# A fused conv and feed-forward block on one core: the pipeline's first three steps put in another order

## The chip, the core and the metric

The kernel runs on one core of a Trainium2 chip. The metric is the device time of one execution in microseconds (us); of several runs the median counts. Six engines work side by side, each with its own instruction stream, and meet only at semaphores: TensorE (PE, with its weight loads as PEld), VectorE (DVE), ScalarE (ACT), GpSimd (POOL) and SyncE (SP). SP and ACT issue the transfers; "SPq" and "ACTq" in a row stand for such issues.

## The reference

For an image batch x of 4 x 48 x 128 x 128 (channels second):

```
x = x + conv(ln_c(x))          # ln_c: mean and variance over the 48 channels of a pixel
  conv: 3x3 conv of the first 12 channels, 1x1 conv 48 -> 254,
        rfft2 of each 8x8 patch * fft_w, irfft2,
        gelu(first 127) * (last 127), 1x1 conv 127 -> 48
t = tokens(x)                  # one token for each pixel
t = t + ffn(ln_t(t))           # 48 -> 192, relu, 192 -> 48, operands rounded to fp8 (5 exponent, 2 mantissa bits)
```

## The kernel before, in words

The work is cut into 32 steps (`STEPS`), each of 16 image rows. A step's data run through a pipeline of seven stages written out in `step(t)` of every engine: a call of `step` for turn a does stage 0 for chunk a, stage 1 for chunk a-1, and so on up to stage 6. So the first turns are a filling in which most stages are not live. In this text turn a is the call for chunk a; (n) behind a name is the chunk.

What a chunk goes through in its first three turns:

- **Stage 0.** SP loads x(n) into `xin` (two slots, so x(2) needs x(0) to be used up), in two halves of 48 channels (`load_x`, L342). ACT copies it in patch order into the single buffer `xord` (`order_x`, L934). PE turns it to pixels in `bank[0]` and `bank[1]` (eight transposes, L784). ACT reads the two banks as `xpix` (L1068) and squares (L1071). DVE makes sums, mean and variance `st` (L1435 to L1459). POOL takes the power -1/2 (`pow`, L1555), copies it to `rm` (L1559), centres the pixels (`centre`, `xcen`, L1530) and scales them into `zpix` (L1572).
- **Scaling of the 12 conv channels.** They lie in another layout (`cx`). For the first three chunks DVE spreads the statistics (`widen_rows`, `tch`, L1193), PE multiplies with masks (`spread(a)`, L595), and DVE applies the result to `cx` (`early_channels`, `cz`, L1206 to L1215). Later chunks get them by way of DRAM (`rm_scratch`).
- **Stages 1 and 2.** SP stores `cz` to DRAM (`store_channels`, L308), into rows between zero rows (`pads`, stored by ACT at the start, L941), and reads it back shifted as `taps` (`load_taps`, L333 and L335). PE does the 3x3 conv (`stream`, L568), ACT copies it out (`convs`, L1114), PE turns it (`convolve`, L577), ACT writes it into `zpix` (L1122).
- **Stage 3.** PE transforms (`fwd`, L803), ACT and DVE split the result into fp16 parts `zh` and `zl`, PE mixes channels (`mix`, L519) and transforms back (`inverse`, L532 and L539), with `gelu` on ACT and `gate` on DVE. Stages 4 to 6 are the projection and the feed-forward part.

The weights are loaded by SP in the same queue and turned by PE in turn 2 (`setup`, L493 to L503). Matmuls on the identity (`keep_busy`, L583) have no use but to occupy PE. The order of work is written out by hand on every engine; each engine stands still at the first wait that is not met. Around the change it is this. PE in turn 2: turn x(2), `spread(1)`, weight setup, 16 `keep_busy`, `stream(0)`, 2 `keep_busy`, `convolve(0)`, `spread(2)`; turn 3 begins with turning x(3), then the transform of chunk 0. SP in turn 2: stores, `cx`, `taps`, then x(3), then biases. POOL in turn 0: power, then `rm`; `centre(0)` follows in turn 1.

Of the kernel before, what the change touches and what calls it, by code (L numbers as in the profile page):

```python
# [80 lines left out]
def metaformer_kernel(nc, x, w_pc, w_in, fft_w, w_out, w1, b1, w2, b2, fwd_d, inv_d, sel_d, eye_d, out):  # L81
    with ExitStack() as ctx:
# [120 lines left out]
        small_set = sem("small_set")  # L203
        zeroed = sem("zeroed")
# [89 lines left out]
        tiles = lambda t: t.rearrange("p (r i w) -> p i r w", r=PATCH, w=TW)  # L294

# [42 lines left out]
        def _(sp):  # L338
# [16 lines left out]

            sp.dma_start(eye[:], eye_d).then_inc(eye_in, 16)
            load_x((0, 0), 0)
            load_cx((0, 0), 0)
            load_x((0, 0), -1)
# [58 lines left out]
            def step(t):  # L418
# [68 lines left out]
        def _(pe):  # L487
# [272 lines left out]

            def step(t):
# [14 lines left out]
                if live(t, 0):  # L776

                    if not peeled:
                        pe.wait_ge(hid16_ready, upto(6 * l + 5))
                    if peeled and a == 0:  # L780
                        pe.wait_ge(eye_in, 16)
                    pe.wait_ge(xord_ready, upto(a + 1))
                    for i in range(PAIRS):
                        mm = pe.transpose(bank[i // 4][:, (i % 4) * 128:(i % 4) * 128 + XSPAN],  # L784
                                          xord[:, i * PX:(i + 1) * PX], eye[0:XSPAN, 0:XSPAN])
                        if i % 4 == 3:
                            mm.then_inc(xT_done, 1)
# [96 lines left out]
        def _(act):  # L884
# [30 lines left out]
            def layers():  # L915

                act.wait_ge(wT, 1)
                act.wait_ge(set_dve, 12 + 4)
# [11 lines left out]
            def order_x(t, behind):  # L930
# [3 lines left out]
                act.activation(xord[:].rearrange("p (i r w) -> p i r w", r=PATCH, w=TW),  # L934
                                tiles(xin[:, ring(t, behind), :]), ACT.Copy).then_inc(xord_ready, 1)

            act.wait_ge(row_zeroed, 1)
            for part in range(2):
                for r in (0, PR - 1):
                    images = cz_d[part].rearrange("c (b r) w -> c b r w", b=BATCH)  # L940
                    act.dma_start(images[:, :, r, :], zero_row[0:CC, :].unsqueeze(1).to_broadcast([CC, BATCH, PW]))\  # L941
                      .then_inc(pads_out, 16)
# [114 lines left out]

            def step(t):
                a, n, m, k, l = (at(t, d) for d in (0, 3, 4, 5, 6))
                filling = isinstance(t[0], int) and t[1] < 3  # L1060
                if live(t, 0):
                    for q in range(2):
                        act.wait_ge(xT_done, upto(2 * a + q + 1))
                        if q == 0:
                            act.wait_ge(xcen_ready, upto(a - 1))
                            act.wait_ge(sum1, upto(a - 1))
                        src = bank[q][:].rearrange("p (i c) -> p i c", c=128)[:, :, 0:XSPAN]
                        act.activation(xpix[:, ring(t, 0), 4 * q:4 * q + 4, :], src, ACT.Copy).then_inc(xpix_ready, 1)  # L1068
                        act.wait_ge(stat1, upto(4 * a))
                        act.sem_inc(act_held, 1)  # L1070
# [579 lines left out]
```

## Time and profile before

| | us |
|---|---|
| median of 3 runs (lowest, highest) | 699.83 (699.67, 700.46) |
| span of the profiled execution | 699.4 |
| PE busy | 666.5 (95% of the span) |
| DVE, ACT, POOL busy | 597.9, 536.8, 456.9 |

The times are of whole executions, the profile is of one more. Its page cuts the span in 40 slices; in the slices' row of PE the first four read 4, 8, 7 and 9 tenths busy, all from there to the last three read 9 (90% or more). So what PE leaves idle lies in the first 70 us or so and at the very end.

### The profile page before, as it was taken

To read this page: it belongs to the slowest core of one execution; us is meant where nothing else is said; L and a number is where in the kernel's file an instruction comes from. 1 tells how busy PE (TensorE), PEld (TensorE's weight loads), DVE (VectorE), ACT (ScalarE), POOL (GpSimd) and SP (SyncE) were. 2 spreads that over 40 slices of the span, in tenths; PEclk is the share of its full clock that TensorE was granted. 3 is DMA by queue.
4 is the path that set the end of the run, shared out by engine and by line. 5 is a ranking of instruction groups with operands and counts; after the bars stand their busy time and mean duration, and the time that the engine had idled before them with its cause. 6 is when DMAs were issued, how large, how long until landed. Compare 5 with 4: busy or idle time off the path is not lost.

```text
span 699.4 us, 19176 instructions
## 1 busy us (share of the span) xinstructions
PE 666.5 (95%) x6620; PEld 529.3 (76%) x6620; DVE 597.9 (85%) x1159; ACT 536.8 (77%) x1087; POOL 456.9 (65%) x347
## 2 busy tenths in 40 slices
PE   4879999999999999999999999999999999999984
PEld 4657877778778877787878877787788777887751
DVE  7637889988988899988988899889888999877877
ACT  4244568888888888888889888888888888877784
POOL 2605677767777777677776877677777876753353
PEclk9989999999999999999999999999999999999995
DMA  4434445444544554445444544545445543342102
GB/s 102 79 78 118 121 113 131 112 126 128 142 120 118 142 140 121 114 120 138 127 123 131 139 131 107 132 121 144 121 116 144 139 129 103 100 119 87 47 23 68
DMA packets 52207, 80.73 MB, mean 115 GB/s; under 512 B 20823, under 2 KB 36079, under 8 KB 52111
## 3 DMA queue, kind: packets, MB, share of 16 engines
q1 hardware_dynamic: 50031, 78.56, 43.2%
q10 hardware_dynamic: 2080, 0.94, 0.6%
q8 instruction: 54, 0.88, 0.6%
q14 instruction: 42, 0.34, 0.2%
HBM read 63.17 MB, written 16.30 MB: 114 GB/s over the span
## 4 chain that ended last, share of the span: by engine, by line
PE 87%; DVE 3%; DMA 3%; issue 2%; ACT 1%; SPq 1%; POOL 1%; DVEq 0%; ACTq 0%; POOLq 0%
PE inva L532 17%; PE invb L539 15%; PE mixp L519 13%; PE misc L548 8%; PE misc L803 8%; PE misc L619 4%; PE misc L519 4%; PE misc L663 3%; PE misc L784 3%; PE misc L568 2%; PE misc L577 2%; PE misc L653 2%; PE mixp L632 2%; PE mixp L639 2%; DMA xin<-in_x_dram 1%
## 5 line engine op out<-in xcount | busy, mean ns | idle before, releaser
L1555 POOL TENSOR_TENSOR st<-st,neg_half 128x16 f32<-128x16 f32 x32 | 93.3, 2915 | 129.2 <-DVE st L1459 129.2
L532 PEld LDWEIGHTS inva<-inv,gmix 128*127 128x127 f32 x1024 | 123.4, 191 | 25.3 <-issue 16.6
L532 PE MATMUL inva<-inv,gmix 128*127 128x128 f32 x1024 | 141.0, 281 | 0.6 <-DVE gmix L1234 0.6
L1234 DVE TENSOR_TENSOR gmix<-mixp,freq_w 128x508 f32<-128x508 f32 x192 | 122.6, 680 | 16.9 <-PE mixp L519 16.9
L539 PE MATMUL invb<-inv,gmix 128*127 128x128 f32 x1024 | 134.7, 274 | 0.1
L539 PEld LDWEIGHTS invb<-inv,gmix 128*127 128x127 f32 x1024 | 126.2, 191 | 2.1 <-DVE hbuf L1245 0.5
L897 ACT ACTIVATE hid<-misc 128x512 f16<-128x512 f32 x180 | 94.1, 599 | 17.7 <-PE misc L619 17.7
L1245 DVE TENSOR_TENSOR hbuf<-gact,invb 127x512 f32<-127x512 f32 x128 | 87.4, 683 | 22.2 <-ACT gact L889 17.7
L1584 POOL TENSOR_TENSOR st<-st,neg_half 128x16 f32<-128x16 f32 x31 | 95.4, 3077 | 16.4 <-DVE st L1313 15.9
L906 ACT ACTIVATE hid<-hid 128x512 fp8e5<-128x512 f16 x174 | 93.2, 619 | 0.0
L889 ACT ACTIVATE gact<-inva 127x512 f32<-127x512 f32 x128 | 77.5, 605 | 19.9 <-PE inva L532 19.3
L519 PE MATMUL mixp<-win,zh 60*128 60x254 f16 x768 | 89.9, 272 | 0.7 <-DVE gmix L1234 0.6
L519 PE MATMUL mixp<-win,zl 60*128 60x254 f16 x768 | 89.0, 267 | 0.0
L1538 POOL TENSOR_TENSOR ob<-tch,y 112x1024 f32<-112x1024 f32 x29 | 62.1, 2140 | 34.1 <-DVE y L1294 34.1
L977 ACT ACTIVATE y<-mixp 112x512 f16<-112x512 f32 x58 | 31.4, 594 | 47.0 <-PE mixp L639 47.0
L803 PE MATMUL misc<-fwd,zpix 128*124 128x128 f32 x512 | 62.1, 275 | 0.0
L548 PE MATMUL misc<-hbuf,wout 127*64 127x512 f32 x248 | 60.1, 605 | 0.0
L803 PEld LDWEIGHTS misc<-fwd,zpix 128*124 128x124 f32 x512 | 58.6, 188 | 0.0
L519 PEld LDWEIGHTS mixp<-win,zh 60*128 60x128 f16 x768 | 37.1, 93 | 26.8 <-issue 14.5
L1435 DVE TENSOR_REDUCE st<-xpix 128x16 f32<-128x768 f32 x32 | 30.5, 952 | 28.3 <-ACT xpix L1068 28.3
L1580 POOL TENSOR_TENSOR tcen<-tpix,st 128x768 f32<-128x768 f32 x31 | 45.7, 1475 | 12.5 <-DVE st L1301 9.6
L1068 ACT ACTIVATE xpix<-misc 128x384 f32<-128x384 f32 x64 | 31.6, 494 | 23.2 <-PE misc L784 22.1
(184 smaller groups left out, 1358.2 us busy)
## 6 DMA issues: line engine op xcount, KB each, us to landing
taps<-cz_scratch SPq DMA_DIRECT2D x63, 292.2 KB
xin<-in_x_dram SPq DMA_DIRECT2D x64, 192.0 KB, 3.3
xres<-in_x_dram SPq DMA_DIRECT2D x64, 192.0 KB, 4.1
out_dram<-ob SPq DMA_DIRECT2D x60, 192.0 KB, 2.6
taps<-cz_scratch SPq DMA_DIRECT2D x63, 146.1 KB
crm<-rm_scratch SPq DMA_DIRECT2D x58, 96.0 KB
cx<-in_x_dram SPq DMA_DIRECT2D x32, 96.0 KB
cz_scratch<-cz SPq DMA_DIRECT2D x63, 48.8 KB
```

The costliest lines, as they stand in the source:

```text
L519: mm = pe.matmul(pair[q][:, e * HID2:(e + 1) * HID2], zpart[r0:r0 + KC, 2 * s + e, :], win[r0:r0 + KC, wpart, :], start=(e == 0 and zpart ...
L532: mm = pe.matmul(inva[0:HID, q * PX:(q + 1) * PX], gmix[:, s % 2, q, 0:HID], inv[:], start=True, stop=True, skip_group_check=True)
L539: mm = pe.matmul(invb[0:HID, q * PX:(q + 1) * PX], gmix[:, s % 2, q, HID:HID2], inv[:], start=True, stop=True, skip_group_check=True)
L548: mm = pe.matmul(dst[HALF * j:HALF * j + HALF, :], wout[:], hbuf[:, half, j, :, :], start=True, stop=True, skip_group_check=True)
L803: mm = pe.matmul(bank[(3, 0)[i // 4]][0:KSPAN, (i % 4) * PX:(i % 4 + 1) * PX], zpix[:, ring(t, 3), i, 0:KSPAN], fwd[:], start=True, stop=True,
L889: act.activation(gact[:, s % 2], inva[0:HID, :], ACT.Gelu).then_inc(gelu_ready, 1)
L897: act.activation(hid16[:, 3 * c + g, :], bank[g][:], ACT.Copy).then_inc(hid16_ready, 1)
L906: act.activation(hid8[:, 3 * c + g, :], hid16[:, 3 * c + g, :], ACT.Copy, saturate=False)\
L1234: dve.tensor_tensor(gmix[:, s % 2, 2 * q:2 * q + 2, 0:HID2], pair[q][:, 0:2 * HID2].rearrange("p (e c) -> p e c", e=2), freq_w[:], ALU.mul ...
L1245: dve.tensor_tensor(hbuf[:, s // 2, :, 2 * e:2 * e + 2, :], gact[:, s % 2].rearrange("p (j i c) -> p j i c", j=2, i=2), invb[0:HID, :].rea ...
L1555: pool.tensor_tensor(st1[:, 6, :], st1[:, 5, :], neg_half[:], ALU.pow).then_inc(pow1, 1)
L1584: pool.tensor_tensor(st2[:, 6, :], st2[:, 5, :], neg_half[:], ALU.pow).then_inc(pow2, 1)
```

## The change

It touches only the first turns (0 to 3) and what stands ahead of them.

- Ahead of turn 0: SP loads the first half of x(0), then the identity, then the first half of x(1). ACT issues the second halves. ACT then does a `Gelu` on 8 elements and only then orders x(0). The zero rows (`pads`) are stored by ACT in turn 1.
- `zpix` is zeroed by POOL, not by DVE.
- x(1) is put in patch order by DVE (`order_second_x`), ahead of its statistics of chunk 0; ACT orders x(0) and x(2), x(3) and on.
- POOL does `centre(0)` ahead of the first power. The copy to `rm` in turns 1 and 2 waits for `spread_in` (the widened rows are written), not for the matmuls on them.
- x(3) is loaded by SP in turn 1, ahead of the stores of `cz`.
- PE in turn 2: 12 `keep_busy`, `spread(2)`, `stream(0)`, turning of x(3), `convolve(0)`. Turn 3 begins with the transform.
- ACT in turn 3: first half of the pixels, `zh` half 0, second half of the pixels, `zh` half 1. DVE in turn 3: `zl` half 0 ahead of the sum over x(3).

```
@@ sync, ahead of turn 0
-            load_x((0, 0), 0)
+            load_first_half(0)
             sp.dma_start(eye[:], eye_d)...
+            load_first_half(1)
             load_cx((0, 0), 0)
-            load_x((0, 0), -1)
@@ sync, step
                     if a == 0:
                         setup()
+                        sp.wait_ge(xord_ready, 2)
+                        load_x((0, 2), -1)
...
-                if a == 2:
-                    sp.wait_ge(xord_ready, 2)
-                    load_x(t, -1)
@@ tensor, step
-                    for i in range(PAIRS): ... transpose ...
+                    if a != 3:
+                        turn_x(t)
...
                 if a == 2:
-                    keep_busy(16, bank[1])
+                    keep_busy(12, bank[1])
+                    spread(2)
                 if live(t, 2):
                     stream(t)
-                    if peeled and a == 2:
-                        keep_busy(2, bank[1])
+                    if a == 2:
+                        turn_x((0, 3))
...
                     convolve(t)
-                    if peeled and a == 2:
-                        spread(2)
@@ scalar, ahead of turn 0
+            load_second_half(0)
+            load_second_half(1)
             act.wait_ge(row_zeroed, 1)
-            (four stores of zero rows)
+            act.activation(gact[0:1, 0, 0:8], zero_row[0:1, 0:8], ACT.Gelu)...
             order_x((0, 0), 0)
@@ scalar, step
+                        if a == 3 and q == 0:
+                            pixels(t, 1)
...
-                if live(t, -1):
+                if live(t, -1) and a != 0:
                     order_x(t, -1)
+                if a == 1:
+                    pads()
@@ vector
-            for tile in (raw_b, cz16, xres, zpix, qpix, win, wout, l1, l2, wpc):
+            for tile in (raw_b, cz16, xres, qpix, win, wout, l1, l2, wpc):
...
+            def order_second_x():
+                dve.wait_ge(x_in[1], 32)
+                dve.wait_ge(xT_done, 2)
+                dve.tensor_copy(strips(xord), tiles(xin[:, 1, :])).then_inc(xord_ready, 1)
+
+            order_second_x()
...
+                if a == 3:
+                    low_parts(t, 0)
@@ gpsimd
-                if a == 1:
-                    centre(t, 1)
+                if a == 0:
+                    centre(t, 0)
...
-                    pool.wait_ge(rmT_done, upto(a))
+                    if a in (1, 2):
+                        pool.wait_ge(spread_in, a)
+                    else:
+                        pool.wait_ge(rmT_done, upto(a))
...
+            pool.memset(zpix[:], 0.0).then_inc(zpix_zeroed, 1)
```

Below are the rows of the instruction order at three places; the rows are program order and tell no times.

PE from the second set of masks (`spread(1)` ends just above) to the transform of chunk 0. `misc<-tch` is `spread(2)`, `misc<-eye,xord` the turning of x(3). Before:

```order
L583 MATMUL misc<-eye 128x128 x16
L568 MATMUL misc<-taps,wpc 32x512 x8
L583 MATMUL misc<-eye 128x128 x2
L577 MATMUL misc<-eye,convs 128x128 x4
L595 MATMUL misc<-tch 96x2x128 x4
L784 MATMUL misc<-eye,xord 128x96 x8
L803 MATMUL misc<-fwd,zpix 124x128 x8
```

And with the change:

```order
L588 MATMUL misc<-eye 128x128 x12
L600 MATMUL misc<-tch 96x2x128 x4
L573 MATMUL misc<-taps,wpc 32x512 x8
L775 MATMUL misc<-eye,xord 128x96 x8
L582 MATMUL misc<-eye,convs 128x128 x4
L813 MATMUL misc<-fwd,zpix 124x128 x8
```

`spread(2)` moved ahead of the stream, and the turning of x(3) moved from behind `spread(2)` to between stream and `convolve`.

POOL in turns 0 and 1. `st<-st,neg_half` is the power. Before:

```order
L1555 TENSOR_TENSOR st<-st,neg_half 128x16
L1559 COPY rm<-st 128x16
L1530 TENSOR_TENSOR xcen<-xpix,st 128x576
L1555 TENSOR_TENSOR st<-st,neg_half 128x16
L1559 COPY rm<-st 128x16
```

And with the change:

```order
L1661 MEMSET zpix 128x2048
L1569 ISA
L1569 TENSOR_TENSOR xcen<-xpix,st 128x576
L1594 TENSOR_TENSOR st<-st,neg_half 128x16
L1601 COPY rm<-st 128x16
L1594 TENSOR_TENSOR st<-st,neg_half 128x16
L1601 COPY rm<-st 128x16
```

The centring of chunk 0 no longer stands between the two powers.

SP from the last weight load to the loads of turn 3. Before:

```order
L380 DMA raw_pc<-in_L_conv_w_pc_dram 36x12x1 x6
L308 DMA cz_scratch<-cz 12x8x260 x3
L347 DMA cx<-in_x_dram 96x1x256
L333 DMA taps<-cz_scratch 72x1x2078
L335 DMA taps<-cz_scratch 36x1x2078
L342 DMA xin<-in_x_dram 48x1024 x2
L386 DMA raw_b<-in_L_ffn_b_dram 128x1
```

And with the change:

```order
L386 DMA raw_pc<-in_L_conv_w_pc_dram 36x12x1 x6
L345 DMA xin<-in_x_dram 48x1024 x2
L311 DMA cz_scratch<-cz 12x8x260 x3
L350 DMA cx<-in_x_dram 96x1x256
L336 DMA taps<-cz_scratch 72x1x2078
L338 DMA taps<-cz_scratch 36x1x2078
L392 DMA raw_b<-in_L_ffn_b_dram 128x1
```

The load of x(3) moved from behind the `taps` to ahead of the stores.

## Rows read from the trace of the kernel before

**Rows 1.** Windows: us, busy us of each engine, PEclk, DMA share, GB/s.

```profile
29.00:33.50 4.50, 4.50 (x25) 4.27 (x24) 3.53 (x11) 2.00 (x10) 4.31 (x4) 0.62 0.60 167
...
39.50:46.60 7.10, 5.92 (x22) 4.72 (x23) 1.11 (x3) 2.33 (x5) 0.00 (x0) 0.52 0.17 42
...
107.00:126.00 19.00, 19.00 (x193) 15.23 (x191) 17.07 (x34) 15.93 (x34) 14.52 (x11) 1.00 0.51 132
```

**Rows 2.** The chain that ended last, 28 to 50 us: start, us, what.

```profile
29.73 0.79 SPq L335
...
31.31 7.76 DMA xin<-in_x_dram
...
39.09 1.06 ACT xord L934
...
40.69 1.11 PE misc L577 x4
41.80 3.41 PE misc L595 x8
45.21 1.28 PE misc L784 x8
46.49 1.91 PE misc L803 x16
48.41 1.34 PE misc L583 x12
```

**Rows 3.** Timeline, 30 to 38 us: start, us, engine, line, operation [idle before].

```profile
31.77 1.55 DVE L1193 TENSOR_TENSOR tch<-rm,tch 128x512 f32<-128x512 f32 x1 [0.23 <-POOL rm L1559]
...
37.17 0.65 PE L568 MATMUL misc<-taps,wpc 108*32 108x512 f16 x8 [2.48 <-DMA taps<-cz_scratch]
```

**Rows 4.** Timeline, 58 to 62 us: the same stages one turn later.

```profile
58.51 0.65 PE L568 MATMUL misc<-taps,wpc 108*32 108x512 f16 x8
...
59.21 0.60 ACT L1114 ACTIVATE convs<-misc 128x512 f32<-128x512 f32 x1 [1.13 <-PE misc L568]
...
60.06 0.66 PE L577 MATMUL misc<-eye,convs 128*128 128x128 f32 x4
...
60.76 0.49 ACT L1122 ACTIVATE zpix<-misc 128x384 f32<-128x384 f32 x1 [0.95 <-PE misc L577]
```

**Rows 5.** Timeline, 0 to 7 us: loads and ACT.

```profile
0.74 0.40 SPq L356 DMA_DIRECT2D eye<-in_identity_dram  x1
...
1.20 0.88 SPq L342 DMA_DIRECT2D xin<-in_x_dram  x2
...
4.84 1.28 ACT L934 ACT_TABLE_LOAD   x1 [4.84 <-issue]
...
6.14 1.06 ACT L934 ACTIVATE xord<-xin 96x1024 f32<-96x1024 f32 x1
```

**Rows 6.** The tile xin, 0 to 60 us: its transfers' time from issue.

```profile
DMA to landing us min/median/max: 3.0/4.2/7.8
```

**Rows 7.** Timeline, 7 to 24 us: PE, DVE and POOL.

```profile
9.63 0.95 DVE L1435 TENSOR_REDUCE st<-xpix 128x16 f32<-128x768 f32 x1 [1.06 <-ACT xpix L1068]
...
10.95 1.51 PE L784 MATMUL misc<-eye,xord 96*128 96x96 f32 x8 [2.10 <-ACT xord L934]
...
12.33 2.92 POOL L1555 TENSOR_TENSOR st<-st,neg_half 128x16 f32<-128x16 f32 x1 [11.89 <-DVE st L1459]
...
15.63 1.15 POOL L1530 TENSOR_TENSOR xcen<-xpix,st 128x576 f32<-128x576 f32 x1
15.64 1.17 DVE L1459 TENSOR_SCALAR st<-st 128x16 f32<-128x16 f32 x1
...
16.96 3.41 POOL L1555 TENSOR_TENSOR st<-st,neg_half 128x16 f32<-128x16 f32 x1 [0.18 <-DVE st L1459]
...
21.61 1.97 PE L595 MATMUL misc<-tch 128*96 128x256 f32 x8 [1.31 <-DVE tch L1193]
```

**Rows 8.** The chain again, 72 to 78 us.

```profile
72.95 4.41 DMA taps<-cz_scratch
```

More of the change, by code:

```diff
@@ L203, in metaformer_kernel @@
         small_set = sem("small_set")
+        zpix_zeroed = sem("zpix_zeroed")
+        table_in = sem("table_in")
         zeroed = sem("zeroed")
@@ L759, in drain, with turn_x @@
                 second_layer_half(1, invb)
+            def turn_x(t):
+                a, l = at(t, 0), at(t, 6)
+                if FIRST <= t[1] < LAST:
+                    pe.wait_ge(hid16_ready, upto(6 * l + 5))
+                elif a == 0:
+                    pe.wait_ge(eye_in, 16)
+                pe.wait_ge(xord_ready, upto(a + 1))
+                for i in range(PAIRS):
+                    mm = pe.transpose(bank[i // 4][:, (i % 4) * 128:(i % 4) * 128 + XSPAN],
+                                      xord[:, i * PX:(i + 1) * PX], eye[0:XSPAN, 0:XSPAN])
+                    if i % 4 == 3:
+                        mm.then_inc(xT_done, 1)
             def step(t):
@@ L776, in step @@
                 if live(t, 0):
[L778 to L787, printed above, removed]
+                    if a != 3:
+                        turn_x(t)
                     if a == 1:
@@ L917, in layers @@
                 act.wait_ge(wT, 1)
-                act.wait_ge(set_dve, 12 + 4)
+                act.wait_ge(set_dve, 11 + 4)
                 for j in range(2):
@@ L933, in order_x, with load_second_half, pads @@
                 act.wait_ge(xT_done, upto(2 * a))
-                act.activation(xord[:].rearrange("p (i r w) -> p i r w", r=PATCH, w=TW),
+                act.activation(strips(xord),
                                 tiles(xin[:, ring(t, behind), :]), ACT.Copy).then_inc(xord_ready, 1)
-            act.wait_ge(row_zeroed, 1)
[L938 to L942, printed above, removed]
+            def load_second_half(n):
+                act.dma_start(xin[CH:2 * CH, n, :], xv[0, n, 1]).then_inc(x_in[n], 16)
+            def pads():
+                for part in range(2):
+                    for r in (0, PR - 1):
+                        images = cz_d[part].rearrange("c (b r) w -> c b r w", b=BATCH)
+                        act.dma_start(images[:, :, r, :], zero_row[0:CC, :].unsqueeze(1).to_broadcast([CC, BATCH, PW]))\
+                          .then_inc(pads_out, 16)
+            load_second_half(0)
+            load_second_half(1)
+            act.wait_ge(row_zeroed, 1)
+            act.activation(gact[0:1, 0, 0:8], zero_row[0:1, 0:8], ACT.Gelu).then_inc(table_in, 1)
             order_x((0, 0), 0)
@@ L1056, in drain, with pixels @@
                            .then_inc(out_stored, 16)
+            def pixels(t, q):
+                a = at(t, 0)
+                act.wait_ge(xT_done, upto(2 * a + q + 1))
+                if q == 0:
+                    act.wait_ge(xcen_ready, upto(a - 1))
+                    act.wait_ge(sum1, upto(a - 1))
+                src = bank[q][:].rearrange("p (i c) -> p i c", c=128)[:, :, 0:XSPAN]
+                act.activation(xpix[:, ring(t, 0), 4 * q:4 * q + 4, :], src, ACT.Copy).then_inc(xpix_ready, 1)
+                act.wait_ge(stat1, upto(4 * a))
+                act.sem_inc(act_held, 1)
+                act.activation(xsq[:, 8 * q:8 * q + 8, :].rearrange("p (i j) c -> p i (j c)", j=2), src, ACT.Square).then_inc(xsq_ready, 1)
             def step(t):
@@ L1060, in step @@
                 filling = isinstance(t[0], int) and t[1] < 3
[L1061 to L1070, printed above, removed]
-                        act.activation(xsq[:, 8 * q:8 * q + 8, :].rearrange("p (i j) c -> p i (j c)", j=2), src, ACT.Square).then_inc(xsq_ready, 1)
+                if live(t, 0) and a != 3:
+                    pixels(t, 0)
+                    pixels(t, 1)
+                if a == 3:
+                    pixels(t, 0)
                 if filling and t[1] == 2:
@@ L1085, in step @@
                                        bank[(3, 0)[q]][0:KSPAN, :], ACT.Copy).then_inc(hi_ready, 1)
+                        if a == 3 and q == 0:
+                            pixels(t, 1)
                 if live(t, 4):
@@ L1127, in setup @@
                 act.wait_ge(zeroed, 1)
+                act.wait_ge(zpix_zeroed, 1)
             run(act, step, setup, 1)
@@ L1167, in setup @@
                 dve.tensor_copy(eye8[:], eye[:], saturate=False).then_inc(set_dve, 1)
-                dve.wait_ge(set_dve, 12 + 5)
+                dve.wait_ge(set_dve, 11 + 5)
                 for base in (0, HALF):
@@ L1182, in late_setup @@
                 dve.tensor_copy(b8[:], raw_b[:], saturate=False).then_inc(set_dve, 1)
[L1183 removed]
+                dve.wait_ge(set_dve, 11 + 11)
                 dve.tensor_copy(bq[:], b8[:]).then_inc(set_dve, 1)
@@ L1186, in late_setup @@
                 dve.tensor_copy(l1h[:], l1[:]).then_inc(set_done, 1)
-                dve.wait_ge(set_dve, 12 + 12)
+                dve.wait_ge(set_dve, 11 + 12)
             def widen_rows(a):
@@ L1429, in step @@
                     early_channels(1)
+                if a == 3:
+                    low_parts(t, 0)
                 if live(t, 0):
@@ L1436, in step @@
                 if live(t, 3):
-                    low_parts(t, 0)
+                    if a != 3:
+                        low_parts(t, 0)
                     low_parts(t, 1)
@@ L1622, in setup @@
                 pool.wait_ge(zeroed, 1)
+                pool.wait_ge(zpix_zeroed, 1)
             run(pool, step, setup, 1)
```

10 lines of the change are left out of this document (6 added, 4 removed).

## The prediction

> **What bounds the kernel now.** I first read the table of busy times over stretches. Between 107 and 126 us PE is busy 19.00 of 19.00 us at a granted clock of 1.00 [rows 1]: from there to the drain the time is PE's work, and this change does not touch that work. So whatever the filling loses or gains moves everything behind it, and the question is only when the full steps begin. I take as that moment the first `mix` of chunk 0, which starts at about 49.7 us (the row of 48.41 us ends there, [rows 2]).
>
> Next I read the chain of what ended last, backwards from that moment, because it names what each engine waited for. It runs, in order: the `taps` issues on SP, the load of x(3) queued behind them (7.76 us from issue, landing at 39.07), ACT ordering x(3), then on PE `convolve` 1.11, `spread(2)` 3.41, turning x(3) 1.28, the transform 1.91 and `keep_busy` 1.34 us [rows 2]. Yet the taps themselves were there at 37.17, when the stream began [rows 3]. From the stream to the first mix thus pass 12.5 us, and most of it is not needed for chunk 0: it is work for x(3) and chunk 2 that stands in the way.
>
> Last I read the first 24 us as a timeline. Each chunk's statistics end in a power of about 3 us on POOL, and two of these in a row, with a centring between them, lead to `spread(1)` at 21.61 [rows 7]. Everything to the stores of `cz` and the issue of the `taps` follows from there.
>
> I call T the start of `stream(0)`, 37.17 us before. The change has three parts: what comes before `spread(1)`, what comes from there to T, and what comes from T to the first mix.
>
> **Part one, up to spread(1).** ACT orders x(0) at 6.14, right as its table load ends (4.84 + 1.28 = 6.12) [rows 5]; that load stood behind four stores of zero rows. After the change two x issues and the table load are over well before x(0) is there, so x(0)'s landing decides. SP's x issues took 0.44 us each [rows 5]; landing takes 3.0 us at least and 4.2 in the median [rows 6]. With the first issue at 0.74 that is 3.7 to 4.9. I take 4.2, near the low end, since nothing is ahead of it in the queues: 1.9 us gained, bounds 1.2 and 2.4. The trace does not show when x(0) landed before, as the table load covers it; at 1.20 + 3.0 = 4.2 it can have been there, so the gain is the cover taken away and hardly the second queue.
>
> The Trainium skill has a rule against the second queue here (DMA: Bandwidth & Descriptors, its decision table): spreading transfers over issuing engines gives no bandwidth, they share the same 16 DMA engines, and only issue time is saved. By that rule the two halves on ACT are worth their issue time alone; a view in which two queues doubled the rate would put the landing near 3 us and the end another 1 us lower. No row here separates the two.
>
> DVE now orders x(1) ahead of its statistics of chunk 0. ACT's copy of the same shape takes 1.06 us [rows 5]; for DVE I take the same as the upper bound and half of it as the lower. It can start once PE has turned x(0): 4.2 + 1.06 of ordering + 1.51 for eight transposes [rows 7] and a hand-over, so DVE is at it from about 6.9 to 8.0. The sums would be ready to start at 9.63 - 1.9 = 7.7 [rows 7], so DVE starts them at 8.0: 1.6 us gained, and the first power moves from 12.33 to 10.7. That x(1) lands by 6.9 is plausible (issued by 2.1, plus 4.2) with 0.6 us to spare.
>
> The second power began 4.63 us after the first (12.33 to 16.96): 2.92 of power, the copy, then the centring of 1.15 us, in which DVE's last small operation of the statistics took 1.17 us in place of 0.17 [rows 7]. With the centring ahead of the first power, what lies between is the power and a copy with their hand-overs, 3.5 us: the second starts at 14.2, a gain of 2.8. The statistics of chunk 1 are no later: PE turns x(1) at 8.1 where it was 10.95 [rows 7], 2.9 us sooner. The centring now runs while DVE sums squares and is done at 10.2; if it holds up one small DVE operation, that costs 0.3. `spread(1)` thus starts at 18.8. Edits that cost nothing here: POOL's zeroing of `zpix` (POOL was idle 11.89 us before its first power; 1.15 us for 576 elements scales to 4.1 us for 2048) and the zero rows on ACT, which lie in its wait for x(2)'s pixels; if they ran over, only the statistics of chunk 2 would feel it, and these wait for DVE.
>
> **Part two, from spread(1) to T.** The stores and the `taps` issues keep their distance to `spread(1)`: 2.8 us sooner. The last issue ended at 30.52 (29.73 + 0.79) [rows 2], now at 27.7. Before, x(3) was queued right behind and shared the wires. The landing without it is bounded by a later turn, 4.41 us from issue [rows 8]: 32.1. But PE must now do `spread(2)` first. That waits for the widened rows, ready at 33.32 before (31.77 + 1.55) [rows 3], now 30.5; the power, the setup work on DVE and POOL's centring ahead of them keep their distances. At 1.97 us [rows 7] `spread(2)` ends at 32.6. The shorter `keep_busy` ends before 30.5. So T = 32.7 against 37.17: 4.5 us gained (2.8 from part one, 1.7 from x(3) out of the way), and two things end within 0.6 us of each other. Bounds of T: 31.7 (x lands soonest and the second power takes 2.92) and 34.1 (`spread(2)` at the lower clock, 3.41 us [rows 2], with all else as said).
>
> **Part three, from T to the first mix.** The terms are those of a turn in which nothing is in the way [rows 4]: stream to `convs` 0.70 (58.51 to 59.21), `convs` to `convolve` 0.85, to the write of `zpix` 0.70, that write with its hand-over 0.60, the transform 1.91 and `keep_busy` 1.34 [rows 2]. The sum is 6.1 us against 12.5, a gain of 6.4. In other words there go: the wait for x(3) with its ordering (2.2), `spread(2)` (3.41) and the turning (1.28), and 0.5 comes back, since the write of `zpix`, hidden under `spread(2)` before, is now waited for. Turning x(3) now fits into the 1.55 us from stream to `convolve`: 0.65 + 0.82 at the full clock. ACT and DVE are not late: with half of the pixels in between, `zh` half 0 is written by T + 4.5 and `zl` half 0 by T + 5.3, before `keep_busy` ends at T + 6.1; the second halves are done by T + 6.9, before the second mix at T + 7.1. The second table load, which before lay ahead of the first gelu, was covered by PE's work; its going gives nothing. x(3) itself must be in `xord` by T + 0.7; loaded about 8 us ahead of the stream's taps, it is.
>
> **The sum.** 4.5 + 6.4 = 10.9 us. The first mix starts at 38.8 instead of 49.7. Later chains (the statistics of chunk 3 by way of DRAM, the taps of chunks 1 and 2) hang on the work of turn 3 and shift with it; chunk 2's scaling is even sooner. The profiled span is 699.4, 0.4 under the median of 699.83; the span should be 688.5 and the time 699.83 - 10.9 = 688.9. The forecast's own range is 687.3 to 690.4.
>
> **Rivals.**
>
> *The lower clock meets the new chain.* Before, after short idle stretches of PE, the granted clock fell: 0.62 on average from 29 to 33.5 us and 0.52 from 39.5 to 46.6, near the lower level of 1.2 GHz [rows 1]. `convolve` took 1.11 us there against 0.66, `spread` 3.41 against 1.97 [rows 2, 4, 7]. If it falls again as PE waits for DVE or the taps around 25 to 32 us, `convolve` costs 0.45 more, the transform about 1.5 and `keep_busy` about 1.0 (their work doubled): 3.0, hence 691.9, and with a slow `spread(2)` up to 693.3. Against it: PE now has work nearly without a gap from about 28 us to T and beyond, where before it stood idle for 2.48 us [rows 3].
>
> The Trainium skill (TensorE: Matmul & The Clock Gate, Part 1) says that a clock fallen after idling comes back with sustained work, and that the phase differs from run to run. The rows agree on fall and return; the phase would make this rival a matter of runs.
>
> *x(3) in front of the stores.* It is issued behind six fine-grained weight loads. If SP's queue stalls there by 2 us, the stores and T follow: 690.9. For it: the same queue is full of small pieces; against: 2 us lie between that issue and the first store.
>
> *The gain stops at turn 3.* If a chain with a time of its own, not hung on the first mix, sets `stream(2)` (the trip of the statistics through DRAM), part three is lost: 699.83 - 4.5 = 695.3. I find no such chain.
>
> *Slower.* If the altered pattern of work leaves PE at the lower level into the first full step, a step of 19.00 us of PE work [rows 1] takes 38: 699.83 - 10.9 + 19 = 707.9. It turns into a loss once over 10.9 us of full-rate work is done at half rate; before, the longest such stretch was about 7 us [rows 1].
>
> *Nothing changes.* The taps land at 37 whatever stands ahead of them and PE's waits only change names: about 699.8. It would need both gains of part three to be covered, against [rows 2].
>
> **How the numbers follow.** Forecast 0.60, lower clock 0.18, queue stall 0.10, gain stopped 0.05, slower 0.04, nothing 0.03. The first three hold 0.88; the range that takes them in, without the last bit of the slow `spread(2)`, is 686.8 to 692.9. A measurement of this kernel tells 0.2% (1.4 us) from no change; all cases but the last two are faster by more than that: 0.93, 0.03, 0.04.
>
> **What would show it.** Right: ordering of x(0) at 4.2; the second power at 14.2; `spread(1)` at 18.8; `spread(2)` ending at 32.6 and the stream right behind it; the first mix 6.1 us after the stream; from there on the same distances as before. Wrong: an ordering of x(0) that waits past 5 us; DVE waiting for x(1); SP's store later than `cz`; a granted clock near 0.5 after T; or a turn 3 to 5 longer than before.

## The result

| | before | after |
|---|---|---|
| median of 4 runs, us | 700.14 (699.67 to 700.97) | 693.65 (693.26 to 696.3) |
| ratio | | 0.9914, 95% interval 0.9899 to 0.9929 |
| span of the profiled execution, us | 699.4 | 692.0 |
| mean granted clock | 0.980 | 0.987 |

The change gives 6.5 us, 0.9%. The forecast was 10.9 us and 688.9; the measured time lies 0.75 us above the upper end of its range. The direction was right, the size was not. Line numbers of the changed kernel are used from here on.

### The profile after

The windows (us; busy us of PE, weight loads, DVE, ACT, POOL; granted clock; DMA share; GB/s) answer to [rows 1]:

```profile
29.00:33.50 4.50, 4.50 (x24) 4.16 (x23) 2.04 (x4) 2.94 (x11) 3.51 (x4) 0.69 0.72 190
36.00:42.00 6.00, 5.22 (x52) 4.47 (x46) 1.62 (x3) 4.10 (x9) 0.00 (x0) 1.00 0.46 92
107.00:126.00 19.00, 19.00 (x200) 15.38 (x200) 17.34 (x34) 15.94 (x33) 13.75 (x12) 1.00 0.50 133
```

The full steps are as before: PE busy 19.00 of 19.00. The filling is where the gain was made. The clock still falls around 30 us (0.50 from 28.4 to 31.7), under `keep_busy`; the second fall, 0.52 from 39.5 us on in before, is gone.

The chain of what ended last, from the stores of `cz` to the first mix, answers to [rows 2] and [rows 3]:

```profile
23.90 3.39 DMA cz_scratch<-cz
...
28.36 7.27 DMA taps<-cz_scratch
...
35.76 0.65 PE misc L573 x8
36.41 0.81 PE misc L775 x8
37.22 0.56 PE misc L582 x4
37.80 0.50 ACT zpix L1150
...
38.54 1.98 PE misc L813 x16
40.52 1.34 PE misc L588 x12
41.86 1.02 PE mixp L524 x16
```

From the stream to the first mix hardly anything stands in the way any more: 35.76 to 41.80, 6.04 us in place of 12.5. But the stream itself waits for the taps until 35.76. The forecast had 4.41 us for the row that reads 7.27.

PE, ACT, DVE and POOL in the first 16 us, from the timeline (start, us, engine, line, operation, idle before it and what ended that), answer to [rows 5] and [rows 7]:

```profile
4.65 1.06 ACT L943 ACTIVATE xord<-xin 96x1024 f32<-96x1024 f32 x1 [1.48 <-DMA xin<-in_x_dram]
...
6.34 1.51 PE L775 MATMUL misc<-eye,xord 96*128 96x96 f32 x8 [6.34 <-DMA eye<-in_identity_dram]
...
7.99 0.69 DVE L1190 COPY xord<-xin 96x1024 f32<-96x1024 f32 x1 [0.41 <-PE misc L775]
...
8.63 0.95 DVE L1473 TENSOR_REDUCE st<-xpix 128x16 f32<-128x768 f32 x1
...
9.94 1.16 POOL L1569 TENSOR_TENSOR xcen<-xpix,st 128x576 f32<-128x576 f32 x1 [7.40 <-DVE st L1480]
...
10.57 0.55 DVE L1491 SCALAR_TENSOR_TENSOR st<-st 128x16 f32<-128x16 f32 x1
...
11.66 0.49 ACT L1086 ACTIVATE xsq<-misc 128x384 f32<-128x384 f32 x1 [1.15 <-DVE st L1498]
11.69 2.91 POOL L1594 TENSOR_TENSOR st<-st,neg_half 128x16 f32<-128x16 f32 x1 [0.59 <-DVE st L1498]
...
15.35 3.40 POOL L1594 TENSOR_TENSOR st<-st,neg_half 128x16 f32<-128x16 f32 x1 [0.32 <-DVE st L1498]
```

x(0) is ordered at 4.65, yet PE begins at 6.34: the row names the identity, which now stands behind half of x(0). `spread(1)` follows at 19.99, where it was at 21.61.

The gain read along the program, as the stream of each chunk: 37.17 to 35.76 (1.4 us), then 58.51 to 50.64 (7.9), 77.50 to 69.80 (7.7), 649.32 to 641.92 (7.4). It is made by the first mix (49.7 to 41.80, 7.9 us), and 0.5 us of it is lost later in steps of 0.2 to 0.3 us that I have not traced.

### The profile page after: what moved, and what is told of

It is laid out like the page before. It is cut to its first block, busy times and chain, and to the rows that moved or that the text cites. A ratio compares the mean times of both kernels' runs of the same rounds, so it can differ in the third digit from the quotient of the medians.

```text
span 692.0 us, 19152 instructions
## 1 busy us (share of the span) xinstructions
PE 662.4 (96%) x6608; PEld 526.0 (76%) x6608; DVE 595.5 (86%) x1159; ACT 534.6 (77%) x1086; POOL 458.5 (66%) x348
## 4 chain that ended last, share of the span: by engine, by line
PE 81%; DMA 7%; DVE 3%; issue 3%; SPq 2%; POOL 2%; ACT 1%; DVEq 0%; POOLq 0%; ACTq 0%
PE inva L537 16%; PE invb L544 14%; PE mixp L524 12%; PE misc L553 8%; PE misc L813 7%; PE misc L624 4%; PE misc L524 4%; DMA taps<-cz_scratch 3%; PE misc L668 3%; PE misc L775 3%; PE misc L573 2%; PE misc L582 2%; DMA cz_scratch<-cz 2%; PE misc L658 2%; PE mixp L637 2%
## 5 line engine op out<-in xcount | busy, mean ns | idle before, releaser
L1622 POOL TENSOR_TENSOR tcen<-tpix,st 128x768 f32<-128x768 f32 x31 | 45.7, 1475 | 12.5 <-DVE st L1337 9.6
L624 PE MATMUL misc<-q,l1h 48*128 48x512 f16 (+1 forms) x187 | 47.0, 384 | 1.6 <-ACT q L1019 1.6
## 6 DMA issues: line engine op xcount, KB each, us to landing
taps<-cz_scratch SPq DMA_DIRECT2D x63, 292.2 KB
taps<-cz_scratch SPq DMA_DIRECT2D x63, 146.1 KB
```

## The experiments

Two things had to be explained: why T, the stream's start, came 1.4 us sooner and not 4.5, and which part of the change carries the gain. Medians are compared with runs of before on the same chip (700.83, 701.41 and 700.15 us in the three groups of runs). All edits are against the changed kernel.

### Who delays the taps: biases, x(4), or x(3)?

Behind the `taps` issues SP now sends the bias pieces and the next loads. e1 moves the biases one turn later:

```diff
-                if isinstance(a, int) and a == 2:
+                if isinstance(a, int) and a == 3:
                     biases()
```

> The changed kernel, but the five small bias loads are issued by SP in turn 3 instead of turn 2, where they stood right behind the taps of chunk 0. Theory A (what is queued behind the taps slows their landing): the taps land 0.5 to 1.5 us sooner than at 35.62 us, stream(0) starts at 34.3 to 35.3 instead of 35.76, and the first mix moves with it from 41.8 to 40.3 to 41.3. Theory B (the landing has its own pace, 7.3 us from the last issue whatever is queued behind): stream(0) stays at 35.7 to 35.8. What came before (spread(1) at 20.0) is the same by both.

It took 700.53 us (one run, span 698.7): in this run the whole gain was gone, most of it not by way of the taps. The stream began at 36.17, and the last issue of taps (28.10) to the stream took 8.07 us, more than the 7.40 of the changed kernel. The edit didn't empty the queue behind the taps: with the biases away, SP issued x(4) at 29.01 in place of 32.44, so more bytes kept the taps company, not fewer. Then the clock fell:

```profile
36.17 0.65 PE L573 MATMUL misc<-taps,wpc 108*32 108x512 f16 x8 [2.64 <-DMA taps<-cz_scratch]
```

```profile
37.40:44.20 6.80, 6.02 (x29) 5.59 (x28) 1.94 (x3) 3.69 (x9) 0.00 (x0) 0.50 0.41 109
```

The first mix came at 45.02, 8.85 us behind the stream where it is 6.04: 2.8 us for a stretch at the lower level of 1.2 GHz. The other loss lies at chunk 2: the stream there came 20.95 us behind that of chunk 1 (53.86 to 74.81) where it is 19.16 (50.64 to 69.80), and a second stretch at 0.50 followed, from 75.0 to 78.4 us.

e2 adds a hold, so that nothing at all follows the taps:

```diff
                     sp.wait_ge(xord_ready, upto(a))
+                    if a == 3:
+                        sp.wait_ge(stream_done, 1)
```

> As the run before, and SP also issues x(4) only once stream(0) is done, so that nothing at all follows the taps in the queues. Theory A: the last taps packets are through by about 33 us, landing at 33.0 to 34.2, and stream(0) starts right behind spread(2), at 34.0 to 34.3; first mix 40.1 to 40.4; whole time 1.3 to 1.7 us under the changed kernel. Theory B: stream(0) stays at 35.7 to 35.8 and the time is the changed kernel's. A third possibility: x(4) now arrives too late for ACT in turn 3 and turn 4 gets longer; then the first mix moves and the second step's does not.

Median 697.23 us of 8 runs (693.63 to 699.19), ratio 0.9944 (0.9918 to 0.9969): slower than the changed kernel by the medians, although the stream was sooner. These windows and the two rows are of e2:

```profile
29.00:33.00 4.00, 2.80 (x19) 2.29 (x19) 1.84 (x3) 2.70 (x11) 3.28 (x4) 1.00 0.72 211
33.00:35.50 2.50, 1.42 (x15) 0.56 (x14) 1.55 (x4) 0.24 (x1) 0.00 (x0) 1.00 0.02 5
```

```profile
34.56 0.65 PE L575 MATMUL misc<-taps,wpc 108*32 108x512 f16 x8 [1.08 <-DVEq L1248]
...
70.67 1.04 PE L575 MATMUL misc<-taps,wpc 108*32 108x512 f16 x8 [3.14 <-DMA taps<-cz_scratch]
```

From just after 33 us the DMA engines are idle (share 0.02 and 5 GB/s in the second window), until the held x(4) is issued at 35.30: that is the end of the taps' transfer with no company. They moved 211 GB/s before, hardly more than in the changed kernel (199 GB/s from 29 to 33). The stream at 34.56 is 6.54 us behind the last issue, against 7.40; with the same hold e6, below, has 7.05. The traces whose biases follow the taps have 6.98 (e8) to 7.51 us (e7), so this distance differs by 0.5 us without any edit to it. The company of the changed kernel costs 0.9 us at most, and part of that can be chance; more company close behind, in e1, went with 8.07.

The second row shows why the whole is slower. The biases, moved to the end of turn 3, stand ahead of turn 4's loads and its store, and the stream of chunk 2 comes 21.15 us behind that of chunk 1, where it is 19.16. PE idles 3.14 us and the clock falls to 0.51 from 69.6 to 76.5. The last step of POOL on `cz` and the store of it, in e2:

```profile
57.06 0.65 POOL L1562 TENSOR_TENSOR cz<-cz 96x256 f16<-96x256 f32 x1
...
59.97 1.61 SPq L311 DMA_DIRECT2D cz_scratch<-cz  x2
```

`cz` is ready at 57.71 and SP stores it 2.3 us later; in the changed kernel 0.1 us lies between (58.85 and 58.95).

e5 puts the load of x(3) back behind the taps, all else as in the change:

```diff
                         setup()
-                        sp.wait_ge(xord_ready, 2)
-                        load_x((0, 2), -1)
...
+                if a == 2:
+                    sp.wait_ge(xord_ready, 2)
+                    load_x(t, -1)
```

> The changed kernel with x(3) loaded where the kernel before loads it, behind the taps. The prediction's view (x(3) shares the wires with the taps and costs them 1.7 us): stream(0) at 37.0 to 37.5. Theory B (it cost the taps nothing, as their landing took 7.3 us from the last issue with and without it): stream(0) stays at 35.7 to 36.0. By both, ACT's ordering of x(3) now waits for x(3) at about 37.5 and stands ahead of the copy convs, so the first mix moves from 41.8 to 44 to 45 and the time rises by 2 to 3 us.

Median 698.42 us of 6 runs (697.56 to 699.16), ratio 0.9963 (0.9944 to 0.9983). Timeline and windows of e5:

```profile
35.59 0.65 PE L574 MATMUL misc<-taps,wpc 108*32 108x512 f16 x8 [1.91 <-DMA taps<-cz_scratch]
...
38.26 1.54 PE L776 MATMUL misc<-eye,xord 96*128 96x96 f32 x8 [2.01 <-ACT xord L944]
```

```profile
37.00:47.20 10.20, 8.17 (x39) 7.80 (x40) 2.33 (x4) 5.69 (x10) 0.00 (x0) 0.50 0.56 147
```

The stream starts at 35.59 with x(3) queued behind the taps, at 35.76 without. From the last issue it is 7.34 us, against 7.40. So taking x(3) away from behind the taps gained nothing: the forecast's 1.7 us for it do not exist. What x(3) holds up is PE, which waits for it and then runs 10 us at half the clock. That stretch is also why the loss is larger than expected before the run: 4.8 us by the medians where 2 to 3 were expected, and a first mix at 47.47 where 44 to 45 was.

e10 halves the taps of chunk 0 in length; the rest of the tile is zeroed ahead of time, so half of that chunk's convolution is left out:

```diff
+            n = TAPS // 2 if c == 0 else TAPS
...
-            eng.dma_start(taps[0:6 * CC, turn, 0:TAPS], both).then_inc(col_in, 16)
+            eng.dma_start(taps[0:6 * CC, turn, 0:n], both).then_inc(col_in, 16)
```

> The changed kernel with the taps of chunk 0 loaded over half their length (0.45 MB instead of 0.9 MB); the rest is zeroed by POOL early on, so chunk 0's conv is left out in part. Theory C (the landing is paced by the 0.9 MB, about 4.6 us of packets, and not by the last issue): the taps land by 33.5 and stream(0) starts at 33.9 to 34.3, right behind spread(2). The prediction's view (4.4 us from the last issue, whatever the size): stream(0) stays at 35.6 to 35.8 or moves by what hangs on the queue behind it alone, 0.5.

691.86 us (one run, span 690.1). Its chain no longer has the taps in it:

```profile
31.27 1.97 PE misc L603 x8
33.24 0.58 PE misc L576 x8
```

The stream starts right behind `spread(2)`. The last issue is at 27.85, 0.5 us sooner than in the changed kernel, the stream 2.5 us sooner: at least 2 us of the landing went with half of the bytes. So the landing is paced at least in part by volume. The page's list of DMA issues gives 292.2 and 146.1 KB for a pair of taps, and two pairs are 877 KB; at the 199 GB/s of the changed kernel's window that is 4.4 us of transfer, an estimate to which the time to begin and to be acknowledged comes. From the first of the four issues (27.39) to the end of the chain's landing (35.62) it is 8.2 us.

### Whether SP's bias pieces merely changed places

e6 keeps the hold of e2, and sends the biases in turn 3 right behind the `taps` issues of that turn, where SP has nothing to do for a while:

```diff
                         load_taps(sp, c, 1)
+                if a == 3:
+                    biases()
```

> As the run with nothing behind the taps, but with the bias loads in SP's idle stretch of turn 3 (43.6 to 49.8 us), not at its end. Theory: that run's stream(0) at 34.56 was a gain of 1.2 us, given back because the bias loads stood ahead of turn 4's stores and pushed stream(2) back; now stream(0) is at 34.4 to 34.7, stream(2) about 19.1 us behind stream(1) as in the changed kernel, and the whole time 0.8 to 1.2 us under it where the clock stays up. Rival: holding x(4) back is what pushed stream(2); then stream(2) is again over 20 us behind stream(1).

Median 693.68 us (692.76 to 697.8, 4 runs), ratio 0.9907 (0.9872 to 0.9942). The streams of chunks 0 to 2 start at 35.24, 50.12 and 69.56: the distance of 21.15 us in e2 is 19.4 again. With the store that waited in e2 this shows that the distance was stretched by the place of the biases. The medians, 693.68 and 697.23, say the same, though their intervals overlap. And the time is that of the changed kernel, where 0.8 to 1.2 us less was expected: emptying the wires behind the taps is worth nothing that can be measured.

In e6, too, the taps are the last thing on the wires. A window and the stream of e6:

```profile
33.75:35.20 1.45, 0.04 (x1) 0.00 (x0) 1.13 (x3) 0.00 (x0) 0.00 (x0) 1.00 0.00 0
```

```profile
35.24 0.65 PE L575 MATMUL misc<-taps,wpc 108*32 108x512 f16 x8 [1.45 <-DMA taps<-cz_scratch]
```

### The order of the identity and x(0)

e3 issues the identity ahead of the first half of x(0):

```diff
-            load_first_half(0)
             sp.dma_start(eye[:], eye_d).then_inc(eye_in, 16)
+            load_first_half(0)
```

> The changed kernel with one exchange: SP issues the identity ahead of the first half of x(0), as the kernel before did. Theory A (the identity, landing at 6.1 us, holds PE's first transposes, not x(0), ordered by 5.71): the identity lands near 3 us, PE starts at 5.8 to 6.0 instead of 6.34, and spread(1) moves from 19.99 to 19.4 to 19.6. Rival: the identity ahead pushes x(0) back by as much (64 KB, 0.3 us and an issue of 0.4), PE starts at 6.2 to 6.5 and nothing is won.

693.44 us (one run, span 691.6), the changed kernel's time. Timeline of e3:

```profile
5.15 1.06 ACT L943 ACTIVATE xord<-xin 96x1024 f32<-96x1024 f32 x1 [1.99 <-DMA xin<-in_x_dram]
...
6.35 1.51 PE L775 MATMUL misc<-eye,xord 96*128 96x96 f32 x8 [6.35 <-ACT xord L943]
```

PE starts at 6.35 instead of 6.34; x(0) is now 0.5 us later and is what PE waits for. The two trade places. The Trainium skill (DMA: Bandwidth & Descriptors, the rules for kernel authors) says that DMAs from several issuing engines share the same DMA engines and save only issue time. e3 does not test this, as it exchanges two loads of one queue. The changed kernel agrees with it so far: two queues at twice the rate would have put x(0)'s landing near 3 us by the prediction's own estimate, and its ordering began at 4.65.

### The parts of the change alone

e8 undoes the order of PE's work in turn 2 alone (x(3) stays early):

```diff
-                    keep_busy(12, bank[1])
-                    spread(2)
+                    keep_busy(16, bank[1])
...
                     convolve(t)
+                    if a == 2:
+                        spread(2)
```

> The changed kernel with PE's order of turn 2 and 3 as before (16 keep_busy, stream, 2 keep_busy, convolve, spread(2), then x(3)); x(3) is still loaded early. Theory (part three of the sum is work on PE that stood in the way, plus the wait for x(3)): stream(0) as in the changed kernel, 34.5 to 35.8 us; from there to the first mix 8.3 us at the full clock and up to 10.2 at the lower one (spread(2) 1.97 or 3.41, turning 0.82 or 1.28 in the way) instead of 6.05; whole time 2.2 to 4 us over the changed kernel. Rival (PE's idle time before the first mix has room for it, only the wait for x(3) mattered): first mix and time stay within 0.5 us.

Median 695.25 us (694.91 to 697.63, 4 runs), ratio 0.9936 (0.9918 to 0.9954). Timeline and windows of e8:

```profile
35.38 1.05 PE L573 MATMUL misc<-taps,wpc 108*32 108x512 f16 x8 [4.20 <-DMA taps<-cz_scratch]
...
38.23 3.52 PE L600 MATMUL misc<-tch 128*96 128x256 f32 x8
```

```profile
34.70:41.50 6.80, 6.12 (x24) 4.25 (x25) 0.00 (x0) 1.09 (x2) 0.00 (x0) 0.50 0.37 101
```

The fall of the clock is part of this. Ahead of the run 8.3 us from the stream to the first mix were expected at the full clock and up to 10.2 at the lower one; it took 10.1. And this execution was the slowest of the four (697.63): by the median e8 is 1.6 us over the changed kernel, under the 2.2 to 4 expected, so its row in the table below is a bad case and not the usual one.

e9 goes the other way: before, with x(3) early, `spread(2)` ahead of the stream and the turning of x(3) behind it, and ACT's and DVE's new order in turn 3, but all ahead of that (queues, table, zero rows, x(1), POOL's order) left as it was. Its diff against the changed kernel has in SP's part, among other edits,

```diff
-            def load_first_half(n):
-                sp.dma_start(xin[0:CH, n, :], xv[0, n, 0]).then_inc(x_in[n], 16)
-
-            load_first_half(0)
             sp.dma_start(eye[:], eye_d).then_inc(eye_in, 16)
-            load_first_half(1)
+            load_x((0, 0), 0)
...
-            order_second_x()
```

> The kernel before with the turn 2 and 3 edits alone: x(3) loaded early, spread(2) ahead of the stream, x(3) turned behind it, the interleaved order on ACT and DVE. Nothing ahead of turn 0 is changed. Theory (the two parts add up): spread(1) at 21.6 as before, stream(0) at 36.3 to 37.3, first mix 6.05 us behind it, 42.4 to 43.4; whole time 1.3 to 2.5 us over the changed kernel, 5.5 to 7 under the kernel before. Rival (the two parts need each other): more than 4 us over the changed kernel.

Median 695.39 us (695.11 to 697.14, 4 runs), ratio 0.9936 (0.9921 to 0.9952). Its chain:

```profile
29.63 7.30 DMA taps<-cz_scratch
...
37.07 0.65 PE misc L567 x8
```

The last issue of taps is 0.1 us sooner than in before, and so is the stream (37.07 against 37.17), with x(3) out of the way and nothing else moved ahead of the taps: the second piece of evidence that x(3) did not delay them. The first mix is at 43.10, 6.03 us behind the stream. Set side by side, from the timelines:

| kernel | T | T to first mix | first mix | lower clock behind T |
|---|---|---|---|---|
| before | 37.17 | 12.5 | 49.7 | 39.8 to 46.6 |
| e5, x(3) late | 35.59 | 11.9 | 47.47 | 37.0 to 47.2 |
| e8, PE's order undone | 35.38 | 10.1 | 45.46 | to 41.5 |
| e9, prologue undone | 37.07 | 6.03 | 43.10 | none |
| after | 35.76 | 6.04 | 41.80 | none |

e9 alone has 4.8 of the 6.5 us. The prologue adds 1.7 by the medians, within the 1.3 to 2.5 expected. x(3)'s early load and PE's order need each other: without the one, 2.2 us at the first mix are left, without the other 4.2, with both and no prologue 6.6. These three are of single executions, and e5's and e8's hold a stretch at the lower clock.

### Runs of one kernel differ, and the clock

The changed kernel once more, unchanged:

> The changed kernel itself once more, beside the next ones on the same chip. Theory (the whole time of one program differs between executions by where PE's granted clock falls in the filling): the first mix at 41 to 42 us, whole times between 693.3 and 696.5 us, the higher ones with the lower mean clock. Rival (the first measurement was a lucky one): median above 697 us.

Median 693.72 us (692.18 to 694.92, 4 runs), ratio 0.9891 (0.9863 to 0.9919). Its streams and a window:

```profile
34.54 0.65 PE L573 MATMUL misc<-taps,wpc 108*32 108x512 f16 x8 [1.26 <-DMA taps<-cz_scratch]
49.42 0.65 PE L573 MATMUL misc<-taps,wpc 108*32 108x512 f16 x8
69.42 0.65 PE L573 MATMUL misc<-taps,wpc 108*32 108x512 f16 x8 [1.99 <-DMA taps<-cz_scratch]
90.27 0.65 PE L573 MATMUL misc<-taps,wpc 108*32 108x512 f16 x8
```

```profile
71.00:74.30 3.30, 3.30 (x18) 3.30 (x17) 1.28 (x2) 0.95 (x2) 2.00 (x3) 0.50 0.80 219
```

T is 1.2 us sooner than in the other execution of the same kernel, though the stretch from last issue to stream differs by 0.2 only (7.17 and 7.40); the rest came earlier, `spread(1)` at 19.55 and PE's start at 5.90 among it. Then 3.3 us at the lower level follow the 1.99 us of waiting at chunk 2, and the step from stream to stream takes 20.85 us where it is 19.24 in the other execution: 1.6 us. The Trainium skill (TensorE: Matmul & The Clock Gate, Part 1) says that the phase of the clock's return differs between runs of one kernel. The two executions show a difference too, but of the fall: the first has its low stretch at 28.4 to 31.7 us, the second at 71.0 to 74.3.

e7 fills PE's wait for the taps with work that nobody uses:

```diff
                     spread(2)
+                    keep_busy(8, bank[1])
```

> The changed kernel with 8 more keep_busy matmuls between spread(2) and stream(0), where PE stood idle for 1.86 us. Theory (a fall of the granted clock after that idle stretch is what makes some executions 2 to 3 us slower): stream(0) and first mix stay within 0.3 us of the changed kernel's, the clock stays up from about 32 us on, and the times gather at 693.3 to 694. Rival (the falls have other causes): the same spread as the changed kernel. If the clock is low while they run, the matmuls take 3.4 us and stream(0) is up to 1.5 us later.

Median 692.70 us (692.03 to 693.21, 4 runs), ratio 0.9881 (0.9861 to 0.990). Windows of e7, from 12 us to the drain:

```profile
12.00:28.00 16.00, 11.43 (x77) 8.87 (x76) 11.48 (x34) 2.98 (x6) 9.94 (x7) 1.00 0.40 72
28.00:32.00 4.00, 2.80 (x22) 2.45 (x21) 2.40 (x5) 2.94 (x11) 3.81 (x4) 1.00 0.70 179
32.00:36.00 4.00, 3.62 (x32) 2.77 (x31) 1.55 (x4) 0.06 (x1) 0.07 (x1) 1.00 0.93 204
36.00:42.00 6.00, 5.22 (x54) 4.75 (x55) 2.14 (x4) 4.56 (x9) 0.00 (x0) 1.00 0.41 98
42.00:674.00 632.00, 626.21 (x6393) 499.44 (x6389) 557.34 (x1063) 510.04 (x1035) 434.80 (x328) 1.00 0.46 118
```

Not one stretch at the lower level until the drain. Two more runs, first e7 joined to e6, then e7 itself again:

> Both edits that looked good: 8 keep_busy matmuls between spread(2) and stream(0), and nothing behind the taps (x(4) held to the end of stream(0), bias loads in SP's idle stretch of turn 3). Theory (the gains add: 0.5 us from the taps' company, 1 us at the median from executions without a fall of the clock): median 692 to 692.6, stream(0) at 34.3 to 35.3. Rival (only the clock matters): 692.5 to 693.2, as with the filling alone.

> The changed kernel with the 8 more keep_busy matmuls, again, with more rounds. Theory (it removes the slower executions): median 692.4 to 693.2 with no execution over 694.5. Rival (the four executions seen were chance): median 693.5 to 694 and single ones at 695 to 696, as the changed kernel has.

e11: median 693.08 us (692.4 to 695.54, 5 runs), ratio 0.9902 (0.9885 to 0.9919). e12: 692.73 us (692.43 to 695.24, 5 runs), ratio 0.9905 (0.9887 to 0.9923). The version with the filled wait has a lower median both times, 0.9 and 1.0 us under the changed kernel's 693.65 and 693.72, but the intervals overlap and one of its nine runs took 695.24. That it is better is likely and not shown. The hold and the moved biases add nothing to it.

## Why the prediction was wrong

**Part three, T to the first mix: right.** 6.1 us forecast, 6.04 measured, 6.03 in e9; 6.4 us of gain forecast, 6.5 measured. Nothing of what could have stretched it happened in the profiled execution: x(3) was there, ACT and DVE were not late, the clock was up.

**Part two, spread(1) to T: the step that failed.** The forecast took "the landing without it is bounded by a later turn, 4.41 us from issue [rows 8]" and booked 1.7 us for x(3) out of the way. Both halves were wrong. First, 4.41 us is counted from the last of four issues on one queue, whose chain in before has the first and the last of them at

```profile
70.52 0.78 SPq L333
...
72.95 4.41 DMA taps<-cz_scratch
77.36 0.14 issue
```

The landing is 6.8 us behind the first issue (two more lie between). In the filling two queues issue at once, so the last issue stands 1.0 us behind the first (27.39 to 28.36), not 2.4, and more of the same transfer is left to do. That accounts for 1.5 us of the 2.9 between 4.41 and 7.27. The forecast had counted it from the end of the last issue, where the row counts from its start, and so gave back 0.8. The other 1.4 us (8.2 against 6.8 from the first issue) are company, by up to 0.9, and something that stays open. That the issue pattern accounts for the 1.5 is worked out from these rows; no run changed it alone. A row "from the last issue" carries over only if the issues before it lie as they do there. Second, x(3) was not the delay (e5: 35.59; e9: 37.07); volume is, by at least 2 us (e10: 33.2). Last issue to stream, from start to start, is 7.44 us before and 7.40 after: a gain of nothing, less than nothing once T is counted from `spread(1)` (15.56 before, 15.77 after). `spread(2)`, forecast to end at 32.6, ended at 33.9 and was not what the stream waited for.

**Part one, up to spread(1): mis-sized, 1.6 us for 2.8.** x(0) was ordered at 4.65 (4.2 forecast, in the bounds). The step that failed is "it can start once PE has turned x(0): 4.2 + 1.06 of ordering": the identity, which PE needs as well and which the change moves back, was costed at nothing. It landed 4.91 us after its issue, at 6.10, while 200 GB/s were being moved; PE began at 6.34, some 1 us later than the sum had it. In e3's one run putting it first didn't help. The centring did hold one small operation of DVE, 0.55 us for 0.17, and it stood in the first power's way: 11.69 us, 10.7 forecast. The second power followed after 3.66 us (3.5 forecast), at 15.35 for 14.2, released by DVE: the squares of chunk 1 had waited 1.15 us until DVE was done with the single `xsq` tile. The order of the terms held; their sum was 1.2 us too good.

**The baseline.** The forecast laid the profiled execution of before, span 699.4, 0.4 us under the median. In every run since, the device time was the span and 1.8 us: 692.0 goes with 693.84, 691.4 with 693.21, 698.7 with 700.53. By the same 1.8 that execution was one of about 701.2 us, 1.1 above the median of four; why, its trace alone can't tell. By spans the gain is 7.4, by medians 6.5.

**The account.** Of the 10.9 us, 1.2 are missing in part one, 1.9 in part two, part three gives 0.1 more, 0.5 are lost between the first mix and the end: 7.4 by spans. The baseline takes 0.9 more: 6.5. The measured time lies another 0.3 higher than these terms say, as before itself came out at 700.14 and not 699.83. The excess over the range is 0.75 us, so any one of part one, part two and the baseline, forecast as measured, would have brought the time inside; the largest of them is part two.

**The rivals.** "The lower clock meets the new chain" was nearest in time (691.9), yet in the changed kernel's profiled execution it didn't happen. The clock did fall, from 28.4 to 31.7 us, but PE then had `keep_busy` alone to do, and `spread(2)` ran at the full clock (1.89 us). But its price was about right where it happened: e1 lost 2.8 us between stream and mix, 3.0 forecast. Where a fall comes differs between executions. x(3) in front of the stores: no stall, SP issued it at 19.52 in 0.89 us, 2 us before the stores. The gain did not stop at turn 3. No case of a slower kernel came up, though e1 hints how near one is: one moved group of issues, and in its one run the whole gain was gone.

**The range** had ends for T (31.7 and 34.1) that both kept the landing of 4.41 us from one later stage, and it never asked what the landing would be if x(3) had not been the delay. The measured distance, 7.4 us from the last issue, stood in the trace of before and would have given T = 34.4 for the forecast's own `spread(1)` (26.9 + 7.44), and 35.6 for the real one.

## What to carry to other kernels

A landing time belongs to the whole group of transfers: count from the first issue, with the bytes beside it, before a row of another stage is carried over, and where a wait is said to come from a neighbour in the queue, keep the measured distance as the other bound. When a change moves one load forward in a queue, write down the new landing of each load that it passed, as the next engine waits for the last of them. Check which of its own runs the profiled execution is before the sum is made against its span.

## What the runs showed of the hardware

- A load can be over for the DMA engines well before the engine that waits for it starts. In e6 they are idle from 33.75 us (0 GB/s), PE is free at 33.8, and the stream, whose row names the taps, starts at 35.24: 1.5 us. In e2 they are idle from 33.25, PE is free at 33.5, and the stream starts at 34.56: 1.3 us. e2's row names DVE as the releaser, but in e10 the stream did not wait for that work of DVE (33.2, with DVE's first step at 33.33). No run was made to measure this by itself.
- What stood idle before the clock fell, from the rows on `stream`: 2.48 us in before, and 2.22 more ahead of `convolve` (its fall at 39.8, in the second of the two), 2.64 in e1, 4.20 in e8, 3.14 in e2 and 1.99 in the repeated run (both at chunk 2), each with a stretch of 3 to 10 us at 0.50 to 0.52 around or behind it. In e5 it was 1.91 us, and 2.01 more before the turning of x(3). After 1.93 us (e3), 1.86 (after), 1.26 (repeated run) and 0.38 us (e7) it stayed at 1.00. With a fall after 1.99 and none after 1.93, the wait alone does not tell the one from the other. The two stretches priced here cost 1.6 us (repeated run) and 2.8 us (e1), about what the prologue brings (1.7 us), or more.
- In the changed kernel DVE copied x(1) (96x1024, f32) in 0.69 us where ACT takes 1.06 for the same shape.
